# All steps of a gated delta-rule attention re-laid in one table per head group

## What is computed

```
qkvz = x @ W_qkvz ; qkv = silu(conv4(qkv)) ; q, k = rmsnorm(q), rmsnorm(k)
M = tril(k_beta @ k.T * decay, -1) ; T = inverse(eye + M)
v_c = T @ v_beta ; k_cumdecay = T @ (k_beta * exp(g))
per chunk: v_new = v_i - kcd_i @ state
           out_i = (q_i * exp(g_i)) @ state + (q_i @ k_i.T * dec_i) @ v_new
           state = state * exp(g_last) + (k_i * ...).T @ v_new
out = (norm_w * rmsnorm(out) * silu(z)) @ W_out
```

## Time and profile before

| | us |
|---|---|
| median of 3 runs | 1412.49 (1408.05 to 1416.64) |
| span of the profiled execution | 1410.6 |
| PE / PEld / DVE / ACT / POOL busy in it | 1289.4 / 901.9 / 1079.0 / 966.9 / 630.6 |
| start of the first unit's inverse (L687) | 71.3 |
| start of the last unit's inverse (L687) | 1099.7 |

### The profile page before, as it was taken

The page is one execution under the profiler, slowest core; times in us unless marked ns, Lnnn a source line. Parts: engine busy times, 40 slices in busy tenths (PEclk is TensorE's granted clock), DMA queues, the critical chain, the costliest instruction groups (busy, mean ns, idle before and its releaser), DMA issues.

```text
span 1410.6 us, 33981 instructions
## 1 busy us (share of the span) xinstructions
PE 1289.4 (91%) x11516; PEld 901.9 (64%) x11516; DVE 1079.0 (76%) x2153; ACT 966.9 (69%) x2129; POOL 630.6 (45%) x726
## 2 busy tenths in 40 slices
PE   3679999999999999999999999999997779999997
PEld 2346676766666676667676766666666546666664
DVE  5587878878797979797888879797966776566565
ACT  2678888897979787978888897979785422222221
POOL 1235445454535354545445554535456378344200
PEclk9899999999999999999999999999999799999999
DMA  3111010101010111101010101010011046454331
GB/s 108 49 31 39 24 39 24 39 24 47 17 47 16 47 43 32 42 24 39 24 39 24 43 20 47 16 47 24 17 40 38 16 136 186 146 157 152 118 99 44
DMA packets 51941, 76.36 MB, mean 54 GB/s; under 512 B 8406, under 2 KB 27256, under 8 KB 51772
## 3 DMA queue, kind: packets, MB, share of 16 engines
q1 hardware_dynamic: 51700, 74.05, 17.5%
q10 hardware_dynamic: 72, 0.14, 0.0%
HBM read 72.85 MB, written 1.32 MB: 53 GB/s over the span
## 4 chain that ended last, share of the span: by engine, by line
PE 62%; DVE 19%; issue 9%; ACT 7%; DMA 1%; DVEq 1%; SPq 0%; POOL 0%; ACTq 0%; POOLq 0%
PE bank L616 12%; PE bank L854 8%; PE products L571 8%; DVE sil L1245 8%; PE products L791 6%; PE products L664 3%; PE products L782 3%; PE products L768 3%; PE bank L696 3%; PE bank L676 3%; DVE u L1318 3%; PE bank L704 3%; DVE t L1305 2%; PE bank L753 2%; PE products L667 2%
## 5 line engine op out<-in xcount | busy, mean ns | idle before, releaser
L616 PE MATMUL bank<-xT,whl 128*128 128x512 f16 x1152 | 309.2, 383 | 11.4 <-DVE sil L1245 11.2
L1245 DVE SCALAR_TENSOR_TENSOR sil<-bank,cw,sil 128x510 f32<-128x510 f32 (+2 forms) x384 | 283.7, 739 | 12.3 <-ACT sil L938 7.0
L1589 POOL COPY t<-eye 128x512 f16<-128x512 f16 x64 | 39.1, 612 | 465.5 <-PE bank L704 465.5
L1305 DVE CAST_PREDICATED t<-levm,bank 128x256 f16<-128x256 uint8 x384 | 166.0, 432 | 94.8 <-PE bank L689 47.0
L1034 ACT ACTIVATE x<-bank 128x256 f16<-128x256 f32 x320 | 125.8, 393 | 101.3 <-PE bank L676 99.3
L1130 ACT ACTIVATE kq<-vtok 128x512 f16<-128x512 f32 x94 | 58.7, 629 | 169.0 <-DVE vtok L1512 168.5
L1318 DVE CAST_PREDICATED u<-levm,bank 128x256 f16<-128x256 uint8 x384 | 163.5, 426 | 0.3
L616 PEld LDWEIGHTS bank<-xT,whl 128*128 128x128 f16 x1152 | 92.7, 98 | 81.8 <-DVE sil L1245 15.9
L676 PEld LDWEIGHTS bank<-t,n 128*128 128x128 f16 x1536 | 82.0, 98 | 94.5 <-DVE t L1305 72.0
L1512 DVE SCALAR_TENSOR_TENSOR vtok<-products,b1s,zs 128x512 f32<-128x512 f32 x94 | 70.4, 749 | 86.3 <-PE products L571 83.2
L676 PE MATMUL bank<-t,n 128*128 128x64 f16 x1536 | 109.6, 194 | 26.1 <-DVE t L1305 24.9
(11 more groups left out here) (209 smaller groups left out, 3223.0 us busy)
## 6 DMA issues: line engine op xcount, KB each, us to landing
grow<-rowsc SPq DMA_DIRECT2D x64, 256.0 KB, 3.4
wt<-wqkvz SPq DMA_DIRECT2D x16, 768.0 KB, 4.5
wms<-wm SPq DMA_DIRECT2D x47, 256.0 KB, 2.8
zs<-gsc SPq DMA_DIRECT2D x36, 256.0 KB, 3.5
wo<-wout SPq DMA_DIRECT2D x16, 256.0 KB, 3.8
zs<-gsc SPq DMA_DIRECT2D x16, 224.0 KB, 3.3
zs<-gsc SPq DMA_DIRECT2D x16, 192.0 KB, 3.2
zs<-gsc SPq DMA_DIRECT2D x18, 160.0 KB, 3.0
```

Source lines behind the costliest of these rows:

```text
L616: mm = nc.tensor.matmul(dst[:, :], whl[:, h, k, col:col + HD], xT[:, l, k, half * 512:(half + 1) * 512], start=(k == 0 and m == 0), stop=( ...
L1245: nc.vector.scalar_tensor_tensor(out=dst[:, :, late:S], in0=src[:, :, 0:S - late], scalar=cw[:, q, i, 3 - late:4 - late], in1=dst[:, :, la ...
L1305: nc.vector.copy_predicated(halves(t16[:, pair(U)], n)[:, :, :, 0], by4(2 * n, n), packed(X_BANK, n)).then_inc(s_tup, 1)
```

## The change

`SLOT` and `FRONT` are replaced by one list `TABLE` with the 385 steps of one group period. Each entry has a step, its level or number, the unit of the group (None for front and end steps) and a lag in groups. Each of the four units has places of its own. The functions that issue the steps, their waits and their buffers are as before. The last group's `end` steps come in the same order of numbers nearly as before, spread through the table. The lines below the table move up by 42: L616 is L574 in the changed kernel, L1034 is L992, L1305 is L1263.

```diff
-SLOT = [("u", 0, 0), ("w", 1, 0), ("sqr", 0, 2), ("exb", 0, 0), ("ss", 0, 2), ("xe", 1, 0), ("x", 2, 0), ("t", 1, 0),
...
-FRONT = {
-    (0, 0): [("rest", 1, 1)],
...
+TABLE = [
+    ("kk", 0, 0, 0), ("end", 32, None, 1), ("acc", 0, 1, 1), ("xe", 4, 3, 1), ("end", 0, None, 1), ("lo", 1, None, 0), ("g", 1, 2, 1),
...
 def sequence():
 
-    for n in range(-2 * B, (HQK + 3) * B):
-        for j in range(len(SLOT) + 1):
-            for part, i, ahead in FRONT.get((n % B, j), ()):
-                g = n // B + ahead
-                if part == "end" and g != HQK - 1:
-                    continue
-                if (-1 if part == "weights" else 0) <= g < HQK:
-                    yield part, i, (None, g)
-                if g == 0 and part == "tap" and i % 3 == 2 and i // 3 < GATES:
-                    yield "gate", i // 3, (None, 0)
-            if j < len(SLOT):
-                what, k, lag = SLOT[j]
-                if 0 <= n - lag < HQK * B:
-                    yield what, k, unit(0, n - lag)
+    for n in range(-4, HQK + 4):
+        for what, k, b, lag in TABLE:
+            g = n - lag
+            if b is not None:
+                if 0 <= g < HQK:
+                    yield what, k, ((None, g), b)
+                continue
+            if what == "end" and g != HQK - 1:
+                continue
+            if (-1 if what == "weights" else 0) <= g < HQK:
+                yield what, k, (None, g)
+            if g == 0 and what == "tap" and k % 3 == 2 and k // 3 < GATES:
+                yield "gate", k // 3, (None, 0)
...
-        FILL_AT = [i for ahead in (2, 1, 0) for key in sorted(FRONT) for s, i, a in FRONT[key]
-                   if s == "fill" and a == ahead]
+        FILL_AT = [k for ahead in range(4, -4, -1) for what, k, b, lag in TABLE if what == "fill" and lag == -ahead]
```

More of the change, by code:

```diff
@@ new lines @@
+TABLE = [
[7 rows of a table added]
+    ("tap", 0, None, -1), ("eye", 0, 1, 0), ("end", 5, None, 1), ("exb", 0, 1, 0), ("x", 1, 0, 0), ("y1", 0, 3, 1), ("xe", 1, 0, 0),
+    ("tap", 1, None, -1), ("sqr", 0, 2, 1), ("w", 1, 0, 0), ("end", 6, None, 1), ("fill", 1, None, -1), ("t", 1, 0, 0), ("hsum", 0, 2, 1),
[6 rows of a table added]
+    ("cap", 0, 1, 0), ("t", 4, 0, 0), ("end", 11, None, 1), ("cap", 1, 1, 0), ("tap", 5, None, -1), ("evict", 2, None, -1),
+    ("u", 4, 0, 0), ("row", 0, 2, 0), ("x", 5, 0, 0), ("kk", 0, 1, 0), ("end", 12, None, 1), ("acc", 0, 2, 1), ("xe", 5, 0, 0),
+    ("exp", 0, 1, 0), ("tap", 6, None, -1), ("cap", 0, 2, 0), ("end", 13, None, 1), ("y1", 1, 3, 1), ("mask", 0, 1, 0), ("cap", 1, 2, 0),
[4 rows of a table added]
+    ("row", 0, 3, 0), ("end", 16, None, 1), ("nl", 0, 1, 0), ("g", 0, 0, 0), ("weights", 1, None, 0), ("tap", 8, None, -1),
+    ("evict", 3, None, -1), ("u", 0, 1, 0), ("tap", 9, None, -1), ("y1", 0, 0, 0), ("eye", 0, 2, 0), ("end", 17, None, 1),
[7 rows of a table added]
+    ("tap", 13, None, -1), ("cap", 1, 3, 0), ("u", 3, 1, 0), ("evict", 5, None, -1), ("tap", 14, None, -1), ("y1", 1, 0, 0),
[3 rows of a table added]
+    ("exb", 0, 3, 0), ("o", 0, 0, 0), ("u", 5, 1, 0), ("evict", 6, None, -1), ("end", 38, None, 1), ("tap", 17, None, -1),
+    ("xe", 6, 1, 0), ("exp", 0, 3, 0), ("nt", 0, 2, 0), ("w", 6, 1, 0), ("fill", 7, None, -1), ("sqr", 0, 0, 0), ("u", 6, 1, 0),
+    ("tap", 18, None, -1), ("n16", 0, 2, 0), ("y0", 0, 1, 0), ("hsum", 0, 0, 0), ("g", 0, 1, 0), ("hz", 0, 0, 0), ("w", 0, 2, 0),
+    ("rest", 7, None, -1), ("t", 0, 2, 0), ("eye", 1, 2, 0), ("tap", 19, None, -1), ("x", 1, 2, 0), ("evict", 7, None, -1),
[22 rows of a table added]
+]
```

90 lines of the change are left out of this document (removed), and 57 rows, old and new, of tables (SLOT, TABLE).

## The result

The changed kernel takes 1430.46 us, median of 7 runs (1423.96 to 1432.47), against 1413.33 for the kernel before beside it. The ratio is 1.0114 with a 95% interval of 1.0085 to 1.0143. I had forecast 1392 and a range up to 1420.

What follows compares the result with a forecast made beforehand. The chain of levels was taken as the bound, lengthened by work in its way. 63.1 + 1.1 = 64.2 us a group; -23 over 15 periods, +3 last group, -1 before the first unit: 1392 us, range 1374 to 1420.

Steps and rivals of the forecast that it cites:

- The walk over PE's places: PE work beyond each level's free room lengthens the four units: 63.1 us a group period against 64.8 before.
- term (3): In ACT's in-order queue, steps wait for results that come late: 1.0 to 1.3 us added per group, bounds 0 and 3.
- the "slower" rival: ACT steps waiting for PE ahead of `xe` or `n16` bound the chain: period 67.2, whole 1437 us, chance 0.17.
- both rivals: Period near 65.5: waits eat the gain (1410 ± 6, chance 0.20); above 66: ACT's queue bounds the chain (1437, 0.17).
- step (2): 30 of 63 ACT table loads go, 2.6 us of ACT per group; no term by itself, as ACT isn't full.
- The last group: Without a next group's front, units take 14.7, 16.1, 15.5 against 14.75 each: +2.0, ACT waits some +1, together +3.
- taken at nothing: Router and start of the expert part, whose steps keep their mutual order: ±2 us, counted as no change.
- at most +5 in the last group: Half clock coming earlier in the last group doubles PE's steps: at most some +5 us, no chance of its own.
- The experts' part is untouched: The experts' part, behind the router and the expert start, was taken as unchanged, with no term in the sum.

Runs made afterwards that it cites:

- run 1: Changed kernel with one DVE step moved: the fourth unit's `nt` behind `u` of the third unit's level 5, not ahead of its `t`; 1411.32 us, ratio 0.9992.
- run 3: Changed kernel with POOL's `sq` written by two memsets that read nothing, the norm of the keys left out; 1413.51 us, single run.
- run 2: Changed kernel with POOL's order alone changed: `nl`, `eye` ahead of `sq`, the fourth unit's `at`, `nl`, `qx` earlier; 1427.20 us, ratio 1.013.
- run 5: Changed kernel with both moves, the edits of run 1 and run 2 together; 1407.77 us, ratio 0.9974.
- run 8: Changed kernel with one more pair of ACT table loads per group, behind the first `silu`; 1469.66 us, single run.
- run 9: Kernel before with the group's first `silu` moved behind the third unit's first gate evict, one pair of table loads less per group; 1418.88 us, single run.
- run 11: run 5 with the third `silu` (of the keys) over only its first 64 of 1024 columns; 1402.37 us, single run.
- run 4: Changed kernel with spare matmuls keeping PE busy from the last group to the experts' start; 1421.41 us, ratio 1.0052.
- run 10: run 6 without the spare matmuls beside `x` and `w` of the last group's levels; 1404.45 us, ratio 0.9937.
- run 12: run 5 with two halves of projections in the third unit cut from three matmuls to one, the gate incomplete; 1405.81 us, single run.
- run 6: Changed kernel with the edits of run 1, run 2 and run 4 together; 1401.24 us, ratio 0.9939.
- run 7: Kernel before with the same spare matmuls as run 4; 1412.23 us, ratio 0.9995.

## Why the prediction was wrong, by its own steps

**The walk over PE's places** was right to 0.3 us in three units where nothing else was in the way, and short of the fourth by 0.5: 14.9 forecast and 14.89 measured, 16.8 and 17.14; the third was forecast at 16.3 and is 16.55 without the collision, the fourth at 15.0 and is 15.54. With both collisions out a period takes 64.43 us, and I had said 64.2. That is partly luck: the walk alone gave 63.1, 1.3 too little, and the 1.1 that I added for waits on ACT filled the gap by a mechanism that the rows don't show.

**The step that failed is the price of the DVE steps.** I took `nt`, `lo`, `nmul` and `ht` at the durations they have in the trace of before, because the operations are unchanged, and never laid POOL's new places beside DVE's. "Operations and waits unchanged" doesn't mean durations unchanged. Of 66.0 - 64.4 = 1.6 us a period, 1.31 is the one `nt` (runs 1 and 3) and the rest the fourth unit, which gave 0.57 in run 2 and keeps 0.24 of it in run 5: 23 us over 15 periods, of the 26 that were missing. The Trainium skill has the rule, on the page "SBUF — State Buffer", section "Who interferes with whom": a DVE instruction with two SBUF inputs contends with a GpSimd instruction that reads SBUF, not with one that only writes it; the shared port pair is an exclusive lock, and the order of issue decides who blocks. The trace agrees: 1.96 us for `nt` behind a reading `sq`, 0.69 beside a writing one. It ends 0.55 us after `sq`, 0.14 sooner than a whole `nt` would, and `hsum` behind `lo` comes out 0.14 sooner in the same way. In the order before, no `nt` of 64 was over 0.693 us; other steps were stretched there (`nl` up to 1.88 us at a median of 1.16, `qx` up to 1.45 at 0.73), so the old durations weren't free of it either. A rival "POOL's new places stand beside DVE's" would, by my estimate, have been worth 1 to 2 us a period on my 64.2, 1407 to 1422, and it was to be had by laying the two new queues side by side.

**Waits in ACT's queue**, term (3), 1.1 us and the mechanism of the "slower" rival: the rows don't show it. The waits give `hsq` 0.9 us a period, where before it was 2.1, and `hrs` 0.6, and PE waits 0.5 us for `n`. The period of 65.99 lies where I had set the marks of both rivals, but by neither's mechanism.

**Table loads**, step (2): "no term by itself" was wrong for the third unit. There a pair costs 2.49 us for 2.6 of loads (run 8). In the second unit of before, taking a pair and a `silu` away gave 0.45 (run 9). How the fall of the third unit from 19.04 to 16.55 divides between its one load less and PE's pieces that were spread wasn't measured, and stays open; my walk gave it all to PE.

**The last group**: +3 was forecast, +6.6 measured. The price was right at the full clock: in run 11, which lacks nothing in this group, the clock is full throughout its three units, and they take 14.81, 16.83 and 15.84 us, +3.2 on before; the clock is the rest. **The end**: "taken at nothing" was wrong by 10.2 us, and I had given the clock at most +5 in the last group and nothing behind it. The half clock came at a worse place: the experts, who need PE all the time, began at half speed, which is 7.4 us at most. The other 2.8 are open; DVE's long `acc` and `xs` beside POOL are the likely place (run 5), and if so, my "The experts' part is untouched" is the same step as in the periods, durations taken over with the operations. Run 4 got 9 us back, some of it in the last group. What decides where the clock falls isn't settled: PE stood still ahead of the last `proj` for 2.22 us in the changed kernel and for 2.09 before, where the clock stayed full. In the changed kernel and runs 1, 2, 3, 5, 8, 10, 11 and 12, whose last groups differ by the two moves at most, the third unit takes 15.84 to 19.58 us.

## What to carry to other kernels

When an order is laid out anew, put DVE's instructions with two SBUF inputs and POOL's that read SBUF side by side for the new order, before any duration is taken from the old trace; one step moved behind two others was worth 1.2% here. A walk over the chain's levels gave unit lengths to 0.0 to 0.5 us, but it holds for durations and a clock that it doesn't itself predict. Where a phase that needs PE all the time follows one that leaves it waiting, look at the granted clock of both: it may be halved where the phase begins (here in the changed kernel, not in the one before), and an untouched phase can take longer for it.

## What the runs showed of the hardware

- POOL waits for DVE as well: `hsum` takes 1.27 us alone, and 2.05 where it starts 0.03 us after a `lo` of 0.95.
- A DVE instruction held up this way shows as busy, not idle: in the list of lines only the mean and the longest duration tell it (728 ns median and 1967 longest for `nt`, before 686 and 693).
- An ACT table load takes 1.28 us, and the next activation starts 0.02 us behind it (run 8); what a pair costs the kernel was 2.49 us of 2.6 in one unit (run 8) and at most 0.45 in another (run 9).
- Spare matmuls of 0.22 us each when they stand in a row, which only keep PE at work, made the changed kernel 0.6% faster (run 4) and the one with both moves 0.35% (run 6, its interval clear of run 5's), and did nothing for the kernel before (run 7).
